# Edge attention of a graph layer: weights read from PSUM, two steps weighed by ScalarE, the bias added by TensorE

## The chip, the cores and the metric

The kernel runs on one core of a Trainium2 chip. The metric is the device time of one execution in microseconds. Times are in microseconds (us) unless marked ns. PE is TensorE, DVE VectorE, ACT ScalarE, POOL GpSimd, and SP the queue of SyncE.

## The reference, cut to what matters

Four layers follow each other: attention over the edges of a graph, a mixture of experts, a relational graph layer, and a second mixture. The change is in the first one only. Its nodes have 256 features in 8 heads, and there are 100,000 edges, sorted by destination.

```python
q = (nfeat @ Wq.T).reshape(n, HEADS, HEAD_DIM) / SCALING
k = (nfeat @ Wk.T).reshape(n, HEADS, HEAD_DIM)
v = (nfeat @ Wv.T).reshape(n, HEADS, HEAD_DIM)
attn = jnp.einsum('ehd,ehd->eh', k[src], q[dst])
attn = attn + attn_bias
m = jax.ops.segment_max(attn, dst, num_segments=n)
a = jnp.exp(attn - m[dst])
s = jax.ops.segment_sum(a, dst, num_segments=n)
a = a / s[dst]
out = jax.ops.segment_sum(v[src] * a[:, :, None], dst, num_segments=n)
return out.reshape(n, FEAT) @ Wo.T
```

## The kernel before

`attention_layer` works on steps of 128 edges, one edge per partition. Sixteen steps are a group (IT), two steps a pair (so 8 PAIRS in a group), and there are 55 groups (G). The instructions are written out by hand for each engine, and engines wait for each other by semaphores alone. There are 57 periods. In period k three groups are in work at once:

- group k: the products of keys and queries and their sums per head (`product`, `sum_heads`);
- group g = k-1: the bias, the running maxima over edges of one destination, and the exponential (`add_bias`, `scan_ahead`, `scan_back`, `chain_rows`, `maxima`, `factor`);
- group c = k-2: the values times the weights, summed per destination and added to the nodes (`weigh`, `sum_pair`, `add`, `rescale`).

POOL gathers the keys and values of each step by an indirect DMA (L278): 16 in a group, into `KV`, which has room for three groups. A buffer is refilled pair by pair, as soon as `sum_pair` has read it. DVE's `product` waits for the gathers four steps at a time.

PE turns the one-hot masks (`turn_masks`), fetches the queries of a pair by a matmul into the PSUM tensor `QP` (`dst_rows`, L379), of which there are three (BANKS = 3), so that `dst_rows` of pair v waits for the product of pair v-3. It turns the scores of a group into the PSUM tensor T (L404), and the exponentials into W (L433), which lies in the same PSUM bank CH as T and the small rows and columns of the softmax. `sum_pair` (L391) sums the weighed values of a pair.

DVE goes through the eight pairs of a period in the order of the loop in its `body`. For each pair: `product` (L454), then what that pair has of the softmax chain, then one `weigh` (L471), then `sum_heads` (L463), then `add` (L493). `weigh` is three pairs ahead of `add` (LEAD = 3): pairs 0 to 2 of the next group are weighed at pair 7, the first of them after a wait for `w_copied`. `add_bias` (L500) adds the bias to T and writes TB in SBUF, which the scan (L505) and `maxima` (L535) read. `weigh` multiplies two steps of values in `KV` by the weights that ACT has copied there.

ACT makes the masks (`distances`, L308, and `masks`, L317), moves them (`to_sbuf`, `move_masks`), and takes the exponential EX (L339) when `maxima` is done; after PE has turned it, ACT copies the weights from W to the last 8 columns of each step in `KV` (L343). `sum_pair` reads these columns too, as the sum of the weights. All of this stands in one order on ACT: what follows the wait for `neg` follows all masks ahead of it.

SP loads runs, bias and links of group k when `maxima` of group k-3 is done.

Of the kernel before, what the change touches and what calls it, by code (L numbers as in the profile page):

```python
# [190 lines left out]
def attention_layer(nc, m, d):  # L191
# [4 lines left out]
    PERIODS = G + 2  # L196
    RING = 3
    QUADS = IT // 4
    BANKS = 3
    LEAD = 3  # L200
    SUMS = 2
    ROW = 2 * FEAT + HEADS
    assert BANKS == RING and PAIRS % BANKS == 2
    with ExitStack() as ctx:
        s = sems(nc, m, "attn", "staged far masks turned turned_sb q_rows product reduced st_turned biased scan rows row_sums rows_l "
                 "cols most neg exp w_turned w_copied rows_f fac_in fac_out fac_less factor rescaled rescale weighted moved sums added "
                 "cleared")
        kv_in = [[new_sem(nc, m, f"attn_kv_in{i}_{q}") for q in range(QUADS)] for i in range(RING)]
        runs_in = [new_sem(nc, m, f"attn_runs_in{i}") for i in range(RING)]
        sb = lambda nm, sh, dt: ctx.enter_context(nc.sbuf_tensor(f"attn_{nm}", sh, dt))  # L210
# [3 lines left out]
        far = sb("far", [P, 4, P], F32)  # L214
        OHT = sb("OHT", [P, IT, P], F32)
        ST = sb("ST", [P, HEADS * IT], F32)
        TB = sb("TB", [P, P], F32)
        A = sb("A", [P, P], F32)
        B = sb("B", [P, P], F32)
        EX = sb("EX", [P, P], F32)  # L220
# [10 lines left out]
        QP = [ctx.enter_context(nc.psum_tensor(f"attn_QP{i}", [P, 2 * FEAT], F32)) for i in range(BANKS)]  # L231
        CH = ctx.enter_context(nc.psum_tensor("attn_CH", [P, 512], F32))
        SP = [ctx.enter_context(nc.psum_tensor(f"attn_SP{i}", [P, 512], F32)) for i in range(SUMS)]
        T, W = CH[:, 0:P], CH[:, P:2 * P]
        row_f, row_l = CH[0:1, 2 * P:3 * P], CH[0:1, 3 * P:4 * P]
        col_f, col_l, pfac = CH[:, P:P + 1], CH[:, P + 1:P + 2], CH[:, 2 * P:2 * P + HEADS]
        query = lambda blk: m.node[:, bass.ds(blk * NUMC + NUMC, FEAT)]
# [7 lines left out]
        with nc.Block() as block:  # L245
# [38 lines left out]
            @block.scalar  # L284
            def _(act):
                def restage(k, i):
                    if has(k, G):
                        act.copy(stage[:, i * IT:(i + 1) * IT], m.idx_src[:, bass.ds(k * IT, IT)]).then_inc(s["staged"], 1)

                def to_sbuf(k, q):  # L290
                    if has(k, G):

                        need(act, s["q_rows"], (k - 1) * PAIRS + (2 * q + 2))
                        act.wait_ge(s["turned"], k * QUADS + (q + 1))
                        act.copy(OHT[:, 4 * q:4 * q + 4, :].rearrange("p a b -> p (a b)"), TP[q % 2][:, 0:512]).then_inc(s["turned_sb"], 1)

                def move_masks(k, i, q):
                    if has(k, G):

                        act.wait_ge(s["reduced"], k * PAIRS + (2 * q + 2))  # L300
                        act.copy(KV[:, i * IT + 4 * q:i * IT + 4 * q + 4, 0:P], OHB[:, 4 * q:4 * q + 4, :]).then_inc(s["moved"], 1)

                def distances(k, q):
                    if has(k, G):

                        need(act, s["masks"], k * QUADS + q)
                        for n in range(4):
                            act.activation(far[:, n, :], m.iota_f[:, :], ACT.Abs, scale=-1.0,  # L308
                                           bias=m.dst_in[:, bass.ds(k * IT + 4 * q + n, 1)]).then_inc(s["far"], 1)

                def masks(k, q):
                    if has(k, G):

                        need(act, s["moved"], (k - 1) * QUADS + (q + 1))
                        need(act, s["turned"], (k - 1) * QUADS + (q + 1))
                        act.wait_ge(s["far"], k * IT + (4 * q + 4))
                        act.activation(OHB[:, 4 * q:4 * q + 4, :], far[:, :, :], ACT.Relu, scale=-1.0, bias=1.0).then_inc(s["masks"], 1)  # L317

                def body(k, i, turn):
                    g, j = k - 1, (i + 2) % 3  # L320
                    to_sbuf(k, 2)
                    if has(g, G):

                        for q in range(QUADS):
                            act.wait_ge(kv_in[j][q], landed(turn, j != 2) * (16 * 4))
                    restage(k + 2, j)
                    distances(k, 3)
                    move_masks(k, i, 0)
                    masks(k, 3)
                    distances(k + 1, 0)  # L330
                    to_sbuf(k, 3)
                    masks(k + 1, 0)
                    distances(k + 1, 1)
                    move_masks(k, i, 1)
                    masks(k + 1, 1)
                    to_sbuf(k + 1, 0)
                    if has(g, G):
                        act.wait_ge(s["neg"], g + 1)
                        act.activation(EX[:, :], B[:, :], ACT.Exp, scale=-1.0).then_inc(s["exp"], 1)  # L339
                        act.wait_ge(s["fac_in"], g + 1)  # L340
                        act.activation(fac[0:1, 2, :], fac[0:1, 1, :], ACT.Exp, scale=-1.0).then_inc(s["fac_out"], 1)
                        act.wait_ge(s["w_turned"], g + 1)
                        act.copy(KV[:, j * IT:(j + 1) * IT, 2 * FEAT:ROW], W.rearrange("p (h s) -> p s h", s=IT)).then_inc(s["w_copied"], 1)  # L343
                    distances(k + 1, 2)
                    move_masks(k, i, 2)
                    to_sbuf(k + 1, 1)
                    masks(k + 1, 2)
                    if has(g, G):
                        act.wait_ge(s["factor"], g + 1)
                        act.copy(FAC[:, :], pfac).then_inc(s["rescaled"], 1)  # L350
                    move_masks(k, i, 3)

                for n in range(2):
                    restage(n, n)
                for q in range(3):
                    distances(0, q)
                    masks(0, q)
                for q in range(2):
                    to_sbuf(0, q)
                every_period(act, body, PERIODS)  # L360

            @block.tensor
            def _(pe):
# [9 lines left out]
                def dst_rows(k, i, blks, v):  # L373
                    if has(k, G) and v < PAIRS:
# [1 line left out]

                        need(pe, s["product"], k * PAIRS + (v + 1 - BANKS))
                        for u in (2 * v, 2 * v + 1):
                            mm = pe.matmul(QP[(2 * i + v) % BANKS][:, (u % 2) * FEAT:(u % 2 + 1) * FEAT], OHT[:, u, :], query(blks[v]),  # L379
                                           start=True, stop=True)  # L380
                        mm.then_inc(s["q_rows"], 1)

                def sum_pair(c, j, v):
                    if has(c, G):
                        pe.wait_ge(s["weighted"], c * PAIRS + (v + 1))
                        if v % 2 == 0:
                            pe.wait_ge(s["moved"], c * QUADS + (v // 2 + 1))

# [6 lines left out]
                def body(k, i, turn):  # L395
# [4 lines left out]
                    if has(g, G):  # L400
                        pe.wait_ge(s["reduced"], (g + 1) * PAIRS)

                        need(pe, s["rescaled"], g)
                        pe.transpose(T, ST[:, :], m.ident[:, :]).then_inc(s["st_turned"], 1)  # L404
                    dst_rows(k, i, to, 1)
                    sum_pair(c, n, 0)
                    turn_masks(k, 2)
# [22 lines left out]
                    if has(g, G):  # L430
                        pe.wait_ge(s["rows_f"], 3 * g + 3)
                        pe.wait_ge(s["exp"], g + 1)
                        pe.transpose(W, EX[:, :], m.ident[:, :]).then_inc(s["w_turned"], 1)  # L433
                    turn_masks(k + 1, 1)
                    sum_pair(c, n, 7)
# [11 lines left out]
            def _(dve):  # L447
                def product(k, i, turn, v):
                    if has(k, G):
                        if v % 2 == 0:  # L450
                            dve.wait_ge(kv_in[i][v // 2], (turn + 1) * (16 * 4))
                        dve.wait_ge(s["q_rows"], k * PAIRS + (v + 1))
                        keys = KV[:, i * IT + 2 * v:i * IT + 2 * v + 2, 0:FEAT]
                        dve.tensor_tensor(keys, keys, QP[(2 * i + v) % BANKS][:, :].rearrange("p (s c) -> p s c", c=FEAT),  # L454
                                          ALU.mult).then_inc(s["product"], 1)

                def sum_heads(k, i, v):
# [7 lines left out]
                                          AX.X, ALU.add).then_inc(s["reduced"], 1)  # L465

                def weigh(c, j, v):
                    if has(c, G) and v < PAIRS:
                        at = j * IT + 2 * v
                        rows = KV[:, at:at + 2, FEAT:2 * FEAT].rearrange("p s (a b) -> p s a b", b=DH)  # L470
                        dve.tensor_tensor(rows, rows, KV[:, at:at + 2, 2 * FEAT:ROW].unsqueeze(3).to_broadcast([P, 2, HEADS, DH]),  # L471
                                          ALU.mult).then_inc(s["weighted"], 1)

                def rescale(c, blks):
# [18 lines left out]
                        dve.scalar_tensor_tensor(acc, acc, m.same[:, bass.ds(c * IT + 2 * v, 1)], SP[v % SUMS][:, 0:NUMC],  # L493
                                                 ALU.mult, ALU.add).then_inc(s["added"], 1)

                def add_bias(g, j, turn):
                    if has(g, G):
                        dve.wait_ge(runs_in[j], landed(turn, j != 2) * (16 * 5))
                        dve.wait_ge(s["st_turned"], g + 1)
                        dve.tensor_tensor(TB[:, :], T, bias[:, j, :], ALU.add).then_inc(s["biased"], 1)  # L500

                def scan_ahead(g, j):
                    if has(g, G):
                        dve.wait_ge(s["biased"], g + 1)
                        dve.tensor_tensor_scan(A[:, :], runs[:, j, 0:P], TB[:, :], -BIG, ALU.add, ALU.max).then_inc(s["scan"], 1)  # L505

                def scan_back(g, j):
                    if has(g, G):
# [13 lines left out]
                def maxima(g, j):  # L522
                    if has(g, G):
# [8 lines left out]
                        dve.scalar_tensor_tensor(B[:, :], runs[:, j, 2 * P:3 * P], col_l, B[:, :], ALU.add, ALU.max).then_inc(s["most"], 1)  # L532
                        dve.tensor_scalar(fac[0:1, 1, :], old, FLOOR, None, ALU.max).then_inc(s["rows_f"], 1)
                        dve.wait_ge(s["most"], 2 * g + 2)
                        dve.scalar_tensor_tensor(B[:, :], B[:, :], FLOOR, TB[:, :], ALU.max, ALU.subtract).then_inc(s["neg"], 1)  # L535
                        dve.wait_ge(s["rows_f"], 3 * g + 2)
                        dve.scalar_tensor_tensor(fac[0:1, 1, :], fac[0:1, 0, :], FLOOR, fac[0:1, 1, :], ALU.max, ALU.subtract).then_inc(s["fac_in"], 1)
                        dve.scalar_tensor_tensor(old, ahead[0:1, IT - 1::IT], lw[0:1, j, HEADS * IT:HEADS * IT + 1],
# [15 lines left out]
                def body(k, i, turn):  # L554
# [3 lines left out]
                    for v in range(PAIRS):  # L558
                        product(k, i, turn, v)
                        if v == 0:  # L560
                            add_bias(g, j, turn)
                            rescale(c, blks)
                        if v == 1:
                            scan_ahead(g, j)
# [2236 lines left out]
```

## Time and profile before

| | |
|---|---|
| median of 3 runs | 4223.15 us (4221.75 to 4224.39) |
| the profiled execution, its own time | 4219.4 us |
| its span | 4217.6 us |
| mean granted clock of PE over the span | 0.889 |
| attention layer, first gather to last weighing | 178.5 to about 1404 us |
| busy over the span | PE 83%, DVE 67%, POOL 55%, ACT 46% |

The shares of the span are means over stages that differ. The layer that is changed is the stretch from about 178 to 1406 us, some 29% of the span, and it is read by itself below. A busy time of POOL in this stretch is the time of the gathers' instructions alone; the time between them is shown as idle, released by "issue" when the profile shows nothing that the engine waited for.

### The profile page before, as it was taken

What the parts mean: (1) busy time and instruction counts of PE and PEld (TensorE: products, weight loads), DVE (VectorE), ACT (ScalarE), POOL (GpSimd) and SP (SyncE); (2) the same over time, 40 slices, a digit from 0 to 9 for tenths busy, and PEclk for the clock granted to TensorE, in tenths of its full rate; (3) what the DMA queues carried; (4) which work ended last, traced back from release to release, by engine and by line L of the source; (5) the groups of instructions that cost most, each with busy time, mean ns of one, the idle gap of its engine ahead of it and who ended that gap; (6) DMA issues with size and microseconds to landing.
All of it is one profiled execution on the core that took longest, in us unless ns stands there. A gap on an engine that the chain in (4) does not pass through costs nothing. (4 is left out here: it accounts for less than half of the span.)

```text
span 4217.6 us, 67721 instructions
## 1 busy us (share of the span) xinstructions
PE 3496.7 (83%) x17983; PEld 2727.1 (65%) x17984; DVE 2818.7 (67%) x7798; ACT 1935.8 (46%) x5274; POOL 2319.3 (55%) x2470
## 2 busy tenths in 40 slices
PE   8788888888888799799989997877878777866793
PEld 4466666666666699799975444655656555645692
DVE  5499999999999655411112222888888888875456
ACT  2355555555555233233322334666666666636230
POOL 5477777777777155400002222777777777737441
PEclk9899999999999999899999998788887888765896
DMA  6677777777777411111113445555565556534446
GB/s 190 200 210 203 202 206 205 207 205 201 203 207 205 151 40 40 56 35 37 35 55 150 178 178 195 170 175 171 168 178 170 168 168 176 160 107 147 122 133 217
DMA packets 266461, 656.43 MB, mean 156 GB/s; under 512 B 52764, under 2 KB 140984, under 8 KB 250408
## 3 DMA queue, kind: packets, MB, share of 16 engines
q0 software_dynamic: 128768, 394.47, 33.2%
q1 hardware_dynamic: 130328, 251.92, 17.4%
q10 hardware_dynamic: 7056, 6.43, 0.4%
q8 instruction: 132, 2.16, 0.2%
q14 instruction: 177, 1.45, 0.1%
HBM read 521.34 MB, written 131.29 MB: 155 GB/s over the span
## 5 line engine op out<-in xcount | busy, mean ns | idle before, releaser
L278 POOL DMA_INDIRECT attn_KV<-kv_tab,attn_stage x880 | 930.1, 1057 | 279.6 <-issue 252.1
L1846 POOL DMA_INDIRECT rel_V<-h_tab,rel_stage x880 | 833.9, 948 | 309.0 <-issue 229.6
L1949 PE MATMUL rel_SP<-rel_V,rel_OH 128*128 128x264 f32 x1760 | 608.5, 483 | 3.6 <-DVE node L2018 1.7
L379 PE MATMUL attn_QP<-node,attn_OHT 128*128 x1760 | 507.4, 414 | 10.2 <-issue 5.5
L391 PE MATMUL attn_SP<-attn_KV 128*128 128x264 f32 x1760 | 494.7, 407 | 20.9 <-DVE node L493 20.3
L1949 PEld LDWEIGHTS rel_SP<-rel_V,rel_OH 128*128 128x128 f32 x1760 | 372.6, 233 | 75.7 <-ACT rel_OH L1884 10.5
L391 PEld LDWEIGHTS attn_SP<-attn_KV 128*128 128x128 f32 x1760 | 344.9, 201 | 94.8 <-issue 37.7
L2018 DVE TENSOR_TENSOR node<-node,rel_SP 128x264 f32 x880 | 366.0, 416 | 50.5 <-PE rel_SP L1949 28.2
L379 PEld LDWEIGHTS attn_QP<-node,attn_OHT 128*128 128x128 f32 x1760 | 334.1, 203 | 61.3 <-issue 14.6
L1740 PE MATMUL pr_H<-WX,pr_YT 128*128 128x512 f32 x784 | 345.3, 593 | 0.0
L454 DVE TENSOR_TENSOR attn_KV<-attn_KV,attn_QP 128x512 f32<-128x512 f32 x440 | 298.0, 677 | 56.0 <-DMA attn_KV<-kv_tab,attn_stage 55.9
L463 DVE TENSOR_REDUCE attn_ST<-attn_KV 128x16 f32<-128x512 f32 x440 | 297.7, 677 | 0.3
L1641 POOL DMA_INDIRECT pr_R<-r_tab,pr_row_of x49 | 49.1, 1002 | 450.6 <-DVE pr_row_of L1699 431.4
L2024 DVE TENSOR_TENSOR rel_V<-rel_V,rel_WB 128x512 f32<-128x512 f32 x440 | 295.7, 673 | 0.0
L471 DVE TENSOR_TENSOR attn_KV<-attn_KV 128x512 f32<-128x512 f32 x440 | 293.6, 677 | 0.0
L1937 PEld LDWEIGHTS rel_QP<-sd,rel_OHT 128*128 128x128 f32 x1760 | 264.9, 224 | 33.2 <-issue 19.6
L308 ACT ACTIVATE attn_far<-iota_f,dst_in 128x128 f32<-128x128 f32 x880 | 281.1, 391 | 3.6
L1937 PE MATMUL rel_QP<-sd,rel_OHT 128*128 x1760 | 266.5, 303 | 15.2 <-ACT rel_OHT L1867 14.9
L1875 ACT ACTIVATE rel_far<-iota_f,dst_in 128x128 f32<-128x128 f32 x880 | 278.5, 388 | 0.0
L1523 ACT ACTIVATE exp_HT<-exp_HB,b 128x128 f32<-128x128 f32 x448 | 127.7, 368 | 301.5 <-PE exp_HB L1461 301.5
L1565 DVE TENSOR_TENSOR exp_R<-exp_RB,exp_bd 128x256 f32<-128x256 f32 x56 | 23.8, 424 | 360.4 <-PE exp_RB L1540 360.4
L1740 PEld LDWEIGHTS pr_H<-WX,pr_YT 128*128 128x128 f32 x784 | 145.7, 191 | 164.4 <-issue 164.4
(393 smaller groups left out, 6761.0 us busy)
## 6 DMA issues: line engine op xcount, KB each, us to landing
rel_OHT<-dst_rows SPq DMA_DIRECT2D x55, 1024.0 KB
h_tab<-pr_H SPq DMA_DIRECT2D x49, 1056.0 KB, 4.0
attn_KV<-kv_tab,attn_stage POOLq DMA_INDIRECT x880, 3.8
rel_V<-h_tab,rel_stage POOLq DMA_INDIRECT x880
pair_Y<-y SPq DMA_DIRECT2D x105, 130.0 KB, 2.1
kv_tab<-qkv_KV SPq DMA_DIRECT2D x49, 256.0 KB, 2.5
mix_Y<-y_out SPq DMA_DIRECT2D x49, 256.0 KB, 4.3
attn_runs<-runs SPq DMA_DIRECT2D x55, 192.0 KB
```

The source lines that it names most:

```text
L278: pool.indirect_dma_start(out=KV[:, i * IT + u, 0:2 * FEAT], out_offset=None, in_=d["kv_tab"][:, :], in_offset=bass.IndirectOffsetOnAxis(a ...
L379: mm = pe.matmul(QP[(2 * i + v) % BANKS][:, (u % 2) * FEAT:(u % 2 + 1) * FEAT], OHT[:, u, :], query(blks[v]), start=True, stop=True)
L391: mm = pe.matmul(SP[v % SUMS][:, 0:NUMC], KV[:, j * IT + u, 0:P], KV[:, j * IT + u, FEAT:ROW], start=(u % 2 == 0), stop=(u % 2 == 1))
L454: dve.tensor_tensor(keys, keys, QP[(2 * i + v) % BANKS][:, :].rearrange("p (s c) -> p s c", c=FEAT), ALU.mult).then_inc(s["product"], 1)
L463: dve.tensor_reduce(ST[:, :].rearrange("p (h s) -> p s h", s=IT)[:, 2 * v:2 * v + 2, :], KV[:, i * IT + 2 * v:i * IT + 2 * v + 2, 0:FEAT]. ...
L471: dve.tensor_tensor(rows, rows, KV[:, at:at + 2, 2 * FEAT:ROW].unsqueeze(3).to_broadcast([P, 2, HEADS, DH]), ALU.mult).then_inc(s["weighte ...
L1740: mm = pe.matmul(HP[g][:, :], f.YT[:, i, k * P:(k + 1) * P], WX[:, k, g * 512:(g + 1) * 512], start=(k == 0), stop=(k == 1))
L1846: pool.indirect_dma_start(out=V[:, i * IT + u, :], out_offset=None, in_=d["h_tab"][:, :], in_offset=bass.IndirectOffsetOnAxis(ap=stage[:, ...
L1937: mm = pe.matmul(QP[q // 2][:, (u % 8) * RH:(u % 8 + 1) * RH], OHT[:, k % 2, u, :], m.sd[:, bass.ds(blks[u // 2] * RH, RH)], start=True, s ...
L1949: pe.matmul(SP[(c * IT + u) % SUMS][:, 0:NUMC], OH[:, j * IT + u, :], V[:, j * IT + u, :], start=True, stop=True).then_inc(s["sums"], 1)
L2018: dve.tensor_tensor(acc, acc, SP[(c * IT + u) % SUMS][:, 0:NUMC], ALU.add).then_inc(s["added"], 1)
L2024: dve.tensor_tensor(rows, rows, weights[:, 2 * v:2 * v + 2, :].unsqueeze(3).to_broadcast([P, 2, HEADS, DH]), ALU.mult).then_inc(s["weighte ...
```

## The change

- The weights W get a PSUM bank of their own (WB). DVE's `weigh` reads the weights from PSUM, through a view of W, and no longer from `KV`. The copy of the weights into `KV` and DVE's wait for it (`w_copied`) stay. PE turns the next exponentials into W only when DVE's weighings of the group before are done.
- To free that bank, `QP` has two tensors and no longer three: `dst_rows` of pair v waits for the product of pair v-2.
- DVE weighs pairs 0 to 6 (OWN = 7). The last pair, steps 14 and 15, is weighed by ACT, with 16 activations (2 steps x 8 heads), each over 128 partitions x 32 columns in place, with the weight as a scale per partition. They stand after `masks(k + 1, 0)` in ACT's order.
- `add_bias` is gone from DVE, and TB with it. PE multiplies the scores by the identity into T and, after a wait for the bias's load, adds the bias by a second matmul with the identity into the same T. The scan and `maxima` read T in PSUM.

```diff
-    BANKS = 3
+    BANKS = 2
+    OWN = PAIRS - 1
...
-        T, W = CH[:, 0:P], CH[:, P:2 * P]
+        WB = ctx.enter_context(nc.psum_tensor("attn_WB", [P, 512], F32))
+        T, W = CH[:, 0:P], WB[:, 0:P]
+        weights = W.rearrange("p (h s) -> p s h", s=IT)
...
+                def weigh_last(c, j):
+                    if has(c, G):
+                        for u in (IT - 2, IT - 1):
+                            at = j * IT + u
+                            for h in range(HEADS):
+                                mm = act.activation(KV[:, at, FEAT + h * DH:FEAT + (h + 1) * DH],
+                                                    KV[:, at, FEAT + h * DH:FEAT + (h + 1) * DH], ACT.Identity,
+                                                    scale=KV[:, at, 2 * FEAT + h:2 * FEAT + h + 1])
+                        mm.then_inc(s["last_weighted"], 1)
...
                     masks(k + 1, 0)
+                    if has(k - 2, G):
+                        act.wait_ge(s["w_copied"], k - 1)
+                    weigh_last(k - 2, (i + 1) % 3)
                     distances(k + 1, 1)
...
-                            mm = pe.matmul(QP[(2 * i + v) % BANKS][:, (u % 2) * FEAT:(u % 2 + 1) * FEAT], OHT[:, u, :], query(blks[v]),
+                            mm = pe.matmul(QP[v % BANKS][:, (u % 2) * FEAT:(u % 2 + 1) * FEAT], OHT[:, u, :], query(blks[v]),
...
-                        pe.wait_ge(s["weighted"], c * PAIRS + (v + 1))
+                        if v < OWN:
+                            pe.wait_ge(s["weighted"], c * OWN + (v + 1))
+                        else:
+                            pe.wait_ge(s["last_weighted"], c + 1)
...
-                        pe.transpose(T, ST[:, :], m.ident[:, :]).then_inc(s["st_turned"], 1)
+                        pe.matmul(T, ST[:, :], m.ident[:, :], start=True, stop=False).then_inc(s["st_turned"], 1)
+                        pe.wait_ge(runs_in[j], landed(turn, j != 2) * (16 * 5))
+                        pe.matmul(T, m.ident[:, :], bias[:, j, :], start=False, stop=True).then_inc(s["biased"], 1)
...
                         pe.wait_ge(s["exp"], g + 1)
+
+                        need(pe, s["weighted"], g * OWN)
                         pe.transpose(W, EX[:, :], m.ident[:, :]).then_inc(s["w_turned"], 1)
...
-                    if has(c, G) and v < PAIRS:
+                    if has(c, G) and v < OWN:
                         at = j * IT + 2 * v
                         rows = KV[:, at:at + 2, FEAT:2 * FEAT].rearrange("p s (a b) -> p s a b", b=DH)
-                        dve.tensor_tensor(rows, rows, KV[:, at:at + 2, 2 * FEAT:ROW].unsqueeze(3).to_broadcast([P, 2, HEADS, DH]),
+                        dve.tensor_tensor(rows, rows, weights[:, 2 * v:2 * v + 2, :].unsqueeze(3).to_broadcast([P, 2, HEADS, DH]),
                                           ALU.mult).then_inc(s["weighted"], 1)
...
-                        dve.tensor_tensor(TB[:, :], T, bias[:, j, :], ALU.add).then_inc(s["biased"], 1)
...
-                        dve.tensor_tensor_scan(A[:, :], runs[:, j, 0:P], TB[:, :], -BIG, ALU.add, ALU.max).then_inc(s["scan"], 1)
+                        dve.tensor_tensor_scan(A[:, :], runs[:, j, 0:P], T, -BIG, ALU.add, ALU.max).then_inc(s["scan"], 1)
...
-                        dve.scalar_tensor_tensor(B[:, :], B[:, :], FLOOR, TB[:, :], ALU.max, ALU.subtract).then_inc(s["neg"], 1)
+                        dve.scalar_tensor_tensor(B[:, :], B[:, :], FLOOR, T, ALU.max, ALU.subtract).then_inc(s["neg"], 1)
```

## Rows read from the trace of the kernel before

**Rows 1.** Windows: us, busy PE, PEld, DVE, ACT, POOL, clock, DMA

```profile
600.00:900.00 300.00, 253.34 (x1210) 193.25 (x1210) 291.41 (x664) 169.92 (x455) 232.92 (x221) 0.95 0.72 205
```

**Rows 2.** The gather's line, 300 to 1300 us, who waits

```profile
L278 POOL DMA_INDIRECT attn_KV<-kv_tab,attn_stage x732: 946/948/1895, 299.8 to 1299.4; - x183
...
  issue: 208.8, 685
...
  DVE attn_KV L454: 29.7, 40
```

**Rows 3.** Groups by line, POOL, 178 to 222 and 2700 to 3300

```profile
L278 POOL DMA_INDIRECT attn_KV<-kv_tab,attn_stage x35 | 33.3, 951 | 22.1 <-ACT attn_stage L288 11.7 <-issue 10.4
...
L1846 POOL DMA_INDIRECT rel_V<-h_tab,rel_stage x480 | 454.4, 947 | 146.2 <-issue 124.9 <-PE rel_SP L1949 21.3
```

**Rows 4.** Timeline (start, us), DVE, one instruction of each period

```profile
221.72 0.42 DVE L544 TENSOR_SCALAR attn_fac<-attn_fac 1x8 f32<-1x8 f32 x1
...
1361.08 0.35 DVE L544 TENSOR_SCALAR attn_fac<-attn_fac 1x8 f32<-1x8 f32 x1
...
1382.12 0.15 DVE L544 TENSOR_SCALAR attn_fac<-attn_fac 1x8 f32<-1x8 f32 x1
```

**Rows 5.** Timeline, DVE and POOL, 704 to 720 us

```profile
704.67 0.68 DVE L471 TENSOR_TENSOR attn_KV<-attn_KV 128x512 f32<-128x512 f32 x1
...
705.28 0.68 DVE L463 TENSOR_REDUCE attn_ST<-attn_KV 128x16 f32<-128x512 f32 x1
...
708.60 0.28 DVE L500 TENSOR_TENSOR attn_TB<-attn_CH,attn_bias 128x128 f32<-128x128 f32 x1
...
708.80 0.42 DVE L480 SCALAR_TENSOR_TENSOR node<-attn_FAC,node 128x256 f32 x1
...
713.99 0.95 POOL L278 DMA_INDIRECT attn_KV<-kv_tab,attn_stage  x1 [0.30 <-issue]
...
714.37 0.68 DVE L471 TENSOR_TENSOR attn_KV<-attn_KV 128x512 f32<-128x512 f32 x1
...
715.24 0.95 POOL L278 DMA_INDIRECT attn_KV<-kv_tab,attn_stage  x1 [0.30 <-issue]
...
719.19 1.88 POOL L278 DMA_INDIRECT attn_KV<-kv_tab,attn_stage  x1 [0.30 <-issue]
...
719.57 0.67 DVE L471 TENSOR_TENSOR attn_KV<-attn_KV 128x512 f32<-128x512 f32 x1
```

**Rows 6.** Timeline, the softmax chain and ScalarE, 700 to 723 us

```profile
700.92 0.29 DVE L535 SCALAR_TENSOR_TENSOR attn_B<-attn_B,attn_TB 128x128 f32<-128x128 f32 x1
...
702.03 0.27 ACT L343 COPY attn_KV<-attn_CH 128x128 f32<-128x128 f32 x1 [0.38 <-PE attn_CH L433]
...
716.99 1.28 ACT L308 ACTIVATE attn_far<-iota_f,dst_in 128x128 f32<-128x128 f32 x4
...
718.68 0.62 ACT L301 CAST attn_KV<-attn_OHB 128x512 f32<-128x512 bf16 x1 [0.42 <-DVE attn_ST L463]
...
722.87 0.31 ACT L339 ACTIVATE attn_EX<-attn_B 128x128 f32<-128x128 f32 x1 [2.43 <-DVE attn_B L535]
```

**Rows 7.** Groups by line and form, ScalarE, whole span

```profile
L308 ACT ACTIVATE attn_far<-iota_f,dst_in 128x128 f32<-128x128 f32 x880 | 281.1, 391 | 3.6
...
L317 ACT ACTIVATE attn_OHB<-attn_far 128x512 bf16<-128x512 f32 x220 | 138.3, 628 | 1.8
...
L2279 ACT ACTIVATE route_Y<-node,route_shift,route_rstd 128x256 f32<-128x256 f32 x49 | 29.2, 597 | 54.8 <-DVE route_shift L2470 54.8
...
L339 ACT ACTIVATE attn_EX<-attn_B 128x128 f32<-128x128 f32 x55 | 17.0, 309 | 112.1 <-DVE attn_B L535 112.1
```

**Rows 8.** Timeline, PE and its readers, 720 to 724 us

```profile
720.87 1.03 PE L379 MATMUL attn_QP<-node,attn_OHT 128*128 x4
...
721.17 0.67 DVE L454 TENSOR_TENSOR attn_KV<-attn_KV,attn_QP 128x512 f32<-128x512 f32 x1
...
724.00 0.67 DVE L454 TENSOR_TENSOR attn_KV<-attn_KV,attn_QP 128x512 f32<-128x512 f32 x1
```

More of the change, by code:

```diff
@@ L198, in attention_layer @@
     QUADS = IT // 4
-    BANKS = 3
+    BANKS = 2
     LEAD = 3
+    OWN = PAIRS - 1
     SUMS = 2
     ROW = 2 * FEAT + HEADS
-    assert BANKS == RING and PAIRS % BANKS == 2
+    assert PAIRS % BANKS == 0
     with ExitStack() as ctx:
@@ L206, in attention_layer @@
                  "cols most neg exp w_turned w_copied rows_f fac_in fac_out fac_less factor rescaled rescale weighted moved sums added "
-                 "cleared")
+                 "cleared last_weighted")
         kv_in = [[new_sem(nc, m, f"attn_kv_in{i}_{q}") for q in range(QUADS)] for i in range(RING)]
@@ L216, in attention_layer @@
         ST = sb("ST", [P, HEADS * IT], F32)
-        TB = sb("TB", [P, P], F32)
         A = sb("A", [P, P], F32)
@@ L453, in product @@
                         keys = KV[:, i * IT + 2 * v:i * IT + 2 * v + 2, 0:FEAT]
-                        dve.tensor_tensor(keys, keys, QP[(2 * i + v) % BANKS][:, :].rearrange("p (s c) -> p s c", c=FEAT),
+                        dve.tensor_tensor(keys, keys, QP[v % BANKS][:, :].rearrange("p (s c) -> p s c", c=FEAT),
                                           ALU.mult).then_inc(s["product"], 1)
@@ L494, in add @@
                                                  ALU.mult, ALU.add).then_inc(s["added"], 1)
[L496 to L499, printed above, removed]
-                        dve.tensor_tensor(TB[:, :], T, bias[:, j, :], ALU.add).then_inc(s["biased"], 1)
                 def scan_ahead(g, j):
@@ L560, in body @@
                         if v == 0:
-                            add_bias(g, j, turn)
                             rescale(c, blks)
```

## The prediction

> **What bounds the kernel now.** I read the windows first. In the changed layer DVE is busy for 291.41 of 300 us, POOL for 232.92, PE for 253.34 and ACT for 169.92 [rows 1]. That looks like a kernel bound by DVE. The gather's own line says something else. Between 300 and 1300 us it has 732 instructions; idle time of POOL before them is given to "issue" 685 times, 208.8 us or 0.30 us each, and DVE waited for their landing 40 times, 29.7 us in all [rows 2]. So POOL never rests: it is always in a gather or between two. Their median is 948 ns, the longest took 1895 [rows 2]; 732 in 1000 us is one every 1.366 us, 0.30 of it between them, so the mean took 1.06 us. Sixteen make a period of 16 x 1.366 = 21.86 us.
>
> The timeline of DVE gives the same period. The one instruction L544 of each period starts at 221.72 us the first time and at 1382.12 the last but one time, 53 periods later: 1160.40 / 53 = 21.89 us [rows 4]. The shortest period, 1361.08 to 1382.12, is 21.04 [rows 4]: there DVE waited for nobody. So DVE has 21.04 us of work and POOL 21.89, and the difference of 0.85 is waiting: 0.65 of it for a gather to land (29.7 us in 45.7 periods). Both must be shortened for the period to fall.
>
> Why is a gather ever longer than 948 ns? The timeline shows which are. The one at 719.19 took 1.88 us, and DVE weighed beside it from 719.57; the one at 715.24 had sums, an add and a product beside it and took 0.95. Not every meeting costs: that at 713.99 also took 0.95, with a weighing from 714.37 [rows 5]. The same line, before the first weighing (178 to 222 us, 35 gathers, with products, sums and scans on DVE), has a mean of 951 ns, and the relational layer, whose weighing reads its weights from PSUM, gathers 480 times at a mean of 947 [rows 3]. `weigh` is here the one long instruction of DVE with both inputs in SBUF; the product reads one from PSUM.
>
> **The weighing from PSUM.** What it takes away is the excess of the gathers. POOL's period becomes 16 x (0.95 + 0.30) = 20.0 us, 1.9 less. DVE's weighing keeps its length: the product, which has the same size and one input in PSUM, took 0.67 [rows 8], and `weigh` 0.68 [rows 5]. Bounds: if the weighing holds up gathers as before, the excess falls only with the one weighing of eight that goes (below); if nothing holds them up, 20.0.
>
> The Trainium skill (SBUF — State Buffer, Who interferes with whom) speaks both ways: a DVE instruction with two SBUF inputs contends with a GpSimd instruction that reads SBUF, but a tensor_tensor was seen not to stall such a DMA, since its descriptors need the write interface (inferred there). By the second, the excess would have another cause and stay, which is the rival of no effect below. The trace bears out the first, by the rows just given.
>
> **What DVE loses.** One weighing of eight: from the start of L471 to that of the next instruction is 705.28 - 704.67 = 0.61 us [rows 5]. `add_bias`: 708.80 - 708.60 = 0.20 [rows 5]. The scan and `maxima` read T from PSUM in place of TB; product and weighing show no difference between the two memories, so I take 0, bounds -0.05 and +0.05. DVE: 21.04 - 0.61 - 0.20 = 20.23 us. It is now the longer of the two, by 0.23.
>
> **What ACT gains.** Sixteen activations of 32 columns with a pointer as scale; the trace has none. An activation of 128 columns without a pointer took 309 ns and one of 512 took 628: 0.83 ns a column. L308, 128 columns and one pointer, took 391 [rows 7], and four of them in a row 1.28 us, so they follow each other by (1.28 - 0.39) / 3 = 0.30 [rows 6]. With 96 columns fewer the spacing is 0.30 - 0.08 = 0.22 us: 16 x 0.22 = 3.5 us a period. ACT is busy 57% of the time [rows 1], 12.4 of 21.9 us, and would have 15.9 of 20.4. The upper bound is L2279, with two pointers, 597 ns for 256 columns [rows 7]: less 224 columns 0.41, nothing overlapped, 16 x 0.41 = 6.6 us. The lower bound is a little over 0.1 (309 less 80 less the overlap of 0.1), 2 us. I take 3.5, since L308 has the same kind of operand.
>
> The place matters more than the sum. The activations stand ahead of `distances(k + 1, 1)` (716.99), and behind these stand the masks and then EX, whose input DVE gives. ACT has slack there: it idled 0.42 us before 718.68 and 2.43 before EX at 722.87, 2.85 in all [rows 6]. That input comes 0.6 us earlier after the change, since the weighing that goes lies between. So EX starts 3.5 - 2.85 + 0.6 = 1.25 us later than it could. Who waits for it? PE turns it, ACT copies it, and DVE's first weighing waits for the copy. Before, the input's instruction started at 700.92, the copy ended at 702.30 [rows 6] and that weighing started at 704.67 [rows 5]: 2.37 us of slack, of which 1.1 is left. No stall. It would begin at (3.5 + 1.1) / 16 = 0.29 us an activation. Behind EX on PE are masks, the last `sum_pair` and `dst_rows` of the next period; each has over 1 us in the rows around 702 to 708, and I put nothing down for them.
>
> **What PE gains.** T was one transpose; now two float32 matmuls of 128 columns. A pair of 256 columns took 1.03 us for four pieces [rows 8], about 0.22 apart, so four pieces of 128 columns cost 0.5 to 0.9, and 0.3 to 0.7 more than now. The wait for the bias holds nothing: SP issued it two periods before. The scan comes more than a whole pair later on DVE. PE is busy 84% of 21.9 us [rows 1], 18.4, and would be for 18.9 of 20.4.
>
> **Two banks for the queries.** `dst_rows` of pair 7 started at 720.87; its new condition, the product of pair 5, ended at 721.17 + 0.67 = 721.84 [rows 8], so it starts about 1 us later at the most. It was needed at 724.00 [rows 8] and would be ready at 722.9. The gap before it is the longest pair (`maxima`), so this hides too. After the change pairs 4 and 6 are short ones on DVE (product, sums, add: 1.6 us) against 1.8 for PE's two matmul pairs; a lag that PE has from a stretch at 1.2 GHz (its granted clock here has a mean of 0.95 [rows 1], which is a tenth of the time at the lower level) will now sometimes show on DVE. POOL's lateness hid it before. I allow 0.17 us a period, bounds 0 and 0.5.
>
> **The sum.** Period 20.23 + 0.17 = 20.40, saved 21.89 - 20.40 = 1.49, times 53 = 79 us. The last two periods have no gathers, and DVE's own 0.8 goes once there in full: 1 us. Together 80. The profiled execution's own time is 4219.4, so 4139.4; the median of the runs lies 3.75 above it, so 4143 us.
>
> **Rivals.**
> - A part is lost (0.15): EX comes later than counted, or PE's shorter lead shows, and DVE stalls 0.4 to 1.2 us a period. For it: three slacks become one thin one at the same time. Against it: each is over 1 us by the rows. In the middle, period 21.2, saved 37, 4187 us.
> - The weighing still holds up the gathers (0.05). The excess of 1.87 keeps 7/8: period 20.0 + 1.64 = 21.64, saved 0.25 x 53 = 13, 4210 us. Against it, the relational layer's 947 ns.
> - No effect (0.03): the excess has nothing to do with DVE: 21.87, about 4222 us.
> - Slower (0.06): the activations make ACT's order the chain. From 0.29 us each, DVE waits at its first weighing, and the gain is eaten at 0.29 + 1.49 / 16 = 0.38. At 0.41 the period is 20.4 + 16 x 0.12 = 22.3, and the time 53 x 0.43 = 23 us more, 4246. For it: no row shows an activation with a pointer as its scale and alone. Against it: L308's spacing.
> - Better than the sum (0.01): DVE shortens by the scans too, and POOL's 20.0 is the bound: saved 100, 4123 us.
>
> **The numbers.** The likeliest case has 0.70: 20.23 to 20.70 a period, 4128 (with the scans' 0.05) to 4160 us. The range of 8 in 10 takes in two thirds of the partial loss: 4128 to 4190. Measurements of this kernel tell 0.2%, 8 us, from no change. Faster by over that: 0.70 + 0.15 + 0.05 + 0.01 = 0.91, of which I take 0.01 off since 4210 is near the bound; same 0.04; slower 0.06.
>
> **What would show it.** Right: gathers at 946 to 955 ns mean in the stretch; waits of POOL for `sum_pair` appear, because it now runs ahead of DVE; DVE's waits for a gather are gone; L544 every 20.3 to 20.6 us; the new activations 0.22 us apart; EX released by ACT's own order. Wrong: gathers still over 1.0 us (the contention isn't the weighing's inputs), DVE idle before its first `weigh` (ACT), or before products and adds (PE).

## The result and the profile after

The changed kernel takes 4147.49 us (median of 4 runs, 4144.23 to 4149.77) against 4222.45 us before: a ratio of 0.9821, 95% interval 0.9804 to 0.9838. Predicted were 4143 us. Measured once more, the same two kernels took 4146.64 and 4225.36 us, ratio 0.9810 (0.9797 to 0.9824). The profiled execution took 4149.8 us, its span 4148.0.

The windows of the changed kernel, with the columns of [rows 1]:

```profile
600.00:900.00 300.00, 264.58 (x1341) 200.75 (x1341) 298.97 (x679) 227.83 (x727) 226.86 (x239) 1.00 0.77 221
```

DVE now has no idle time to speak of (298.97 of 300 us, 291.41 before), PE's granted clock in the layer is 1.00 where it was 0.95, and ACT is busy for 227.83 us in place of 169.92.

The gather's line (a line number of this kernel), 300 to 1300 us, and what POOL was idle for, to be held against [rows 2]:

```profile
L280 POOL DMA_INDIRECT attn_KV<-kv_tab,attn_stage x785: 944/946/1213, 299.3 to 1289.4; - x197
...
  issue: 231.3, 739
...
  PE attn_SP L409: 12.8, 42
```

There are 785 gathers in the same 1000 us in place of 732; the median is 946 ns and the longest 1213, where it had been 1895. Under "who waited for it" this answer has no line any more: DVE never waits for a gather to land. One sign that the prediction named hardly shows: POOL's waits for `sum_pair` (L409) are 12.8 us at 42 places, 0.30 each, which is the usual time between two gathers, and the kernel before had 14.3 us at 47.

The one instruction of each period, in DVE's timeline, the first and the 54th, as in [rows 4]:

```profile
223.07 0.15 DVE L560 TENSOR_SCALAR attn_fac<-attn_fac 1x8 f32<-1x8 f32 x1
...
1304.77 0.15 DVE L560 TENSOR_SCALAR attn_fac<-attn_fac 1x8 f32<-1x8 f32 x1
```

(1304.77 - 223.07) / 53 = 20.41 us a period; it was 21.89. The 53 periods took 1160.4 us and take 1081.7, 79 us less, and the layer from its first gather to its last `add` is shorter by as much (1228.4 us before, 1149.2 now). The whole was 75 us shorter the first time and 79 the second. In the spans of the two profiled executions the difference is 69.6: the stages behind the layer, which have the same code, took 2819.1 us from the last `add` to the end of the span, where they had taken 2810.7. That difference isn't explained; the repeated run below says a little more.

A stretch of one period in the timeline of the changed kernel, where L310 is the new weighing on ACT, L476 the product, L485 the sum, L551 the input of EX, L354 EX, L356 the small exponential for the factor, L358 the copy of the weights, L560 `factor`, L493 DVE's weighing, L394 the queries' matmuls, L385 the turning of the masks:

```profile
707.02 3.48 ACT L310 ACTIVATE attn_KV<-attn_KV 128x32 f32<-128x32 f32 x16
...
709.13 0.67 DVE L476 TENSOR_TENSOR attn_KV<-attn_KV,attn_QP 128x512 f32<-128x512 f32 x1
...
709.83 0.69 DVE L485 TENSOR_REDUCE attn_ST<-attn_KV 128x16 f32<-128x512 f32 x1
...
712.21 0.29 DVE L551 SCALAR_TENSOR_TENSOR attn_B<-attn_B,attn_CH 128x128 f32<-128x128 f32 x1
...
713.22 0.31 ACT L354 ACTIVATE attn_EX<-attn_B 128x128 f32<-128x128 f32 x1
...
713.42 0.19 ACT L356 ACTIVATE attn_fac<-attn_fac 1x8 f32<-1x8 f32 x1
...
713.97 0.27 ACT L358 COPY attn_KV<-attn_WB 128x128 f32<-128x128 f32 x1 [0.35 <-PE attn_WB L455]
...
714.29 0.35 DVE L560 TENSOR_SCALAR attn_fac<-attn_fac 1x8 f32<-1x8 f32 x1
...
716.00 0.68 DVE L493 TENSOR_TENSOR attn_KV<-attn_KV,attn_WB 128x512 f32<-128x512 f32 x1
...
722.32 1.13 PE L394 MATMUL attn_QP<-node,attn_OHT 128*128 x4 [0.49 <-DVE attn_KV L476]
...
725.27 0.40 PE L385 MATMUL attn_TP<-ident_b,attn_OHB 128*128 128x128 bf16 x4 [0.72 <-ACT attn_OHB L329]
```

Sixteen activations took 3.48 us, the last one's own 0.31 included: (3.48 - 0.31) / 15 = 0.211 us apart. EX starts 1.01 us after the start of its input's instruction; it is ACT's own order now that releases it. Before the change it was 0.33, from the line below to EX at 722.87 [rows 6]. The copy of the weights ends at 714.24, and the first weighing starts at 716.00. PE waits 0.49 us for a product before `dst_rows`, which is the shorter lead of two banks, and only 0.72 us for the masks. Its wait for masks had been 90.1 us at 46 places between 300 and 1300 us.

The input of EX in the kernel before (L535 there is L551 here):

```profile
722.54 0.29 DVE L535 SCALAR_TENSOR_TENSOR attn_B<-attn_B,attn_TB 128x128 f32<-128x128 f32 x1
```

The waits of the same kernel, 300 to 1300 us (total us, times, longest):

```profile
POOL attn_KV L280 <- issue: 231.3, 739, 1.3
...
PE attn_QP L394 <- DVE attn_KV L476: 45.4, 98, 0.5
...
PE attn_TP L385 <- ACT attn_OHB L329: 35.6, 49, 0.8
```

No wait of DVE is among them.

### The profile page after: what moved, and what is told of

It reads as the page before. It is cut to its first block and busy times, and to the rows that moved or that the text cites. A ratio compares the mean times of both kernels' runs of the same rounds, so it can differ in the third digit from the quotient of the medians.

```text
span 4148.0 us, 68767 instructions
## 1 busy us (share of the span) xinstructions
PE 3473.8 (84%) x18148; PEld 2705.6 (65%) x18149; DVE 2773.1 (67%) x7688; ACT 2103.1 (51%) x6154; POOL 2226.9 (54%) x2470
## 5 line engine op out<-in xcount | busy, mean ns | idle before, releaser
L280 POOL DMA_INDIRECT attn_KV<-kv_tab,attn_stage x880 | 836.7, 951 | 285.7 <-issue 259.4
L394 PE MATMUL attn_QP<-node,attn_OHT 128*128 x1760 | 487.2, 400 | 62.7 <-DVE attn_KV L476 56.7
L409 PE MATMUL attn_SP<-attn_KV 128*128 128x264 f32 x1760 | 467.5, 389 | 1.3 <-DVE node L515 1.3
L394 PEld LDWEIGHTS attn_QP<-node,attn_OHT 128*128 128x128 f32 x1760 | 304.8, 192 | 148.4 <-issue 117.2
L409 PEld LDWEIGHTS attn_SP<-attn_KV 128*128 128x128 f32 x1760 | 330.3, 191 | 52.2 <-issue 2.3
L476 DVE TENSOR_TENSOR attn_KV<-attn_KV,attn_QP 128x512 f32<-128x512 f32 x440 | 297.5, 676 | 23.7 <-DMA attn_KV<-kv_tab,attn_stage 23.2
L485 DVE TENSOR_REDUCE attn_ST<-attn_KV 128x16 f32<-128x512 f32 x440 | 298.2, 678 | 2.2
L493 DVE TENSOR_TENSOR attn_KV<-attn_KV,attn_WB 128x512 f32<-128x512 f32 x385 | 254.2, 672 | 0.0
```

Of the source, the lines that this page charges most:

```text
L280: pool.indirect_dma_start(out=KV[:, i * IT + u, 0:2 * FEAT], out_offset=None, in_=d["kv_tab"][:, :], in_offset=bass.IndirectOffsetOnAxis(a ...
L394: mm = pe.matmul(QP[v % BANKS][:, (u % 2) * FEAT:(u % 2 + 1) * FEAT], OHT[:, u, :], query(blks[v]), start=True, stop=True)
L409: mm = pe.matmul(SP[v % SUMS][:, 0:NUMC], KV[:, j * IT + u, 0:P], KV[:, j * IT + u, FEAT:ROW], start=(u % 2 == 0), stop=(u % 2 == 1))
L476: dve.tensor_tensor(keys, keys, QP[v % BANKS][:, :].rearrange("p (s c) -> p s c", c=FEAT), ALU.mult).then_inc(s["product"], 1)
L485: dve.tensor_reduce(ST[:, :].rearrange("p (h s) -> p s h", s=IT)[:, 2 * v:2 * v + 2, :], KV[:, i * IT + 2 * v:i * IT + 2 * v + 2, 0:FEAT]. ...
```

## The experiments

All of them change `attention_layer` alone. "Layer's period" is worked out as above, from the first and the 54th `factor` of the profiled execution.

| kernel | time, us | before on the same chip | ratio (95%) | period, us |
|---|---|---|---|---|
| before | 4222.5 | | | 21.89 |
| changed | 4147.5 | 4222.5 | 0.9821 (0.9804-0.9838) | 20.41 |
| e1 weights from SBUF again | 4163.9 | 4221.6 | 0.9859 (0.9836-0.9882) | 20.88 |
| e2 weights from PSUM alone | 4178.6 | 4221.6 | 0.9899 (0.9883-0.9916) | 21.04 |
| e3 DVE weighs all pairs | 4169.8 | 4221.6 | 0.9876 (0.9860-0.9893) | 20.83 |
| e4 bias on DVE | 4154.5 | 4221.6 | 0.9839 (0.9823-0.9856) | 20.59 |
| changed, repeated | 4146.6 | 4225.4 | 0.9810 (0.9797-0.9824) | 20.41 |
| e8 pair 6 weighed later | 4138.4 | 4225.4 | 0.9794 (0.9781-0.9808) | 20.27 |
| e9 and a third step on ACT | 4126.5 | 4225.4 | 0.9764 (0.9751-0.9777) | 20.15 |
| e5 two banks alone | 4673.2 | 4672.4 | 1.0001 (0.9992-1.0011) | - |
| e6 eight activations more | 4687.3 | 4672.4 | 1.0038 (1.0024-1.0051) | - |
| e7 sixteen activations more | 4697.1 | 4672.4 | 1.0054 (1.0037-1.0072) | - |
| f6 as e6 | 4200.7 | 4225.6 | 0.9936 (0.9920-0.9953) | 21.42 |
| f7 as e7 | 4330.7 | 4225.6 | 1.0246 (1.0229-1.0263) | 23.9 |

**e1, the weights read from SBUF again.**

```diff
-                        dve.tensor_tensor(rows, rows, weights[:, 2 * v:2 * v + 2, :].unsqueeze(3).to_broadcast([P, 2, HEADS, DH]),
+                        dve.tensor_tensor(rows, rows, KV[:, at:at + 2, 2 * FEAT:ROW].unsqueeze(3).to_broadcast([P, 2, HEADS, DH]),
```

> The changed kernel, but DVE's weighing reads the weights from the copy in KV (SBUF) again; everything else of the change stays. Theory (a weighing with both inputs in SBUF lengthens the gathers): the gathers' mean goes from 0.95 back to 1.04-1.06 us, POOL is the bound again with a period of about 21.6 us, and the time is 4147 + 53 x 1.25 = about 4213 us. Rival (the excess had another cause, and DVE's shorter work made the gain): gathers stay at 0.95 us, period 20.4, time 4147 us.

Its gathers by line and by source, 300 to 1200 us:

```profile
L280 POOL DMA_INDIRECT attn_KV<-kv_tab,attn_stage x693 | 690.7, 997 | 211.2 <-issue 198.7 <-PE attn_SP L409 12.5
```

```profile
L280 POOL DMA_INDIRECT attn_KV<-kv_tab,attn_stage x693: 946/947/1530, 299.2 to 1199.8; - x174
...
  DVE attn_KV L476: 15.8, 25
```

The direction is the theory's: the gathers' mean rises to 997 ns, the longest is 1530, and DVE waits for gathers again (15.8 us). The size is not: 4164 us where 4213 were expected, a mean of 0.997 where it was to be 1.04 to 1.06. The rival, no effect, is out: the four runs of e1 lie apart by more than usual (4156.8 to 4174.8 us), but all are above those of the changed kernel. Three meetings of a weighing (L493) and a gather in the timeline of e1 show what the size hangs on:

```profile
335.37 0.68 DVE L493 TENSOR_TENSOR attn_KV<-attn_KV 128x512 f32<-128x512 f32 x1
...
335.65 1.22 POOL L280 DMA_INDIRECT attn_KV<-kv_tab,attn_stage  x1 [0.30 <-issue]
...
338.35 0.67 DVE L493 TENSOR_TENSOR attn_KV<-attn_KV 128x512 f32<-128x512 f32 x1
...
338.43 1.41 POOL L280 DMA_INDIRECT attn_KV<-kv_tab,attn_stage  x1 [0.30 <-issue]
...
710.21 0.95 POOL L280 DMA_INDIRECT attn_KV<-kv_tab,attn_stage  x1 [0.30 <-issue]
...
710.33 0.68 DVE L493 TENSOR_TENSOR attn_KV<-attn_KV 128x512 f32<-128x512 f32 x1
```

The gathers at 335.65 and 338.43 began while a weighing was running, and took 1.22 and 1.41 us; they end about 0.8 us after the weighing did. The gather at 710.21 began 0.12 us before the weighing, and took its 0.95. I counted this over all gathers of the timeline between 300 and 1200 us. In e1, 153 of 692 began in a running weighing and took 1.17 us on average, the other 539 took 0.948. Before, 181 of 657 did and took 1.23; the others took 0.957, but for 23 that took twice a gather's time, 1.88, as the one at 719.19 [rows 5]. So one part of the price is set by how often a gather's start falls into a weighing, 4.4 times a period before and 3.5 in e1, and by how early in the weighing it falls. That depends on how the two engines' rhythms lie to each other, and I had no ground to carry 7/8 of the old excess over.

The other part are the 23. In the timeline each of them began during the product of pair 4, 0.38 to 0.39 us ahead of the weighing of pair 7. Of the 28 gathers that began at this place 23 took 1.88 us, while 28 that began as long ahead of the weighing of pair 5 took 0.95, as the one at 713.99 [rows 5]. e5 (below), which also weighs from SBUF, has the same: 27 of 29 ahead of pair 7's weighing, and none of 19 ahead of pair 5's. Pair 7 is the one that the change gives to ACT, so e1 lacks the place. Of the 78 us by which the 657 gathers before exceeded 0.946 us each, 22 belong to the weighing of pair 7. That is 29%, where the 7/8 had reckoned with one eighth. Why a gather is lengthened ahead of this weighing and not ahead of pair 5's is open.

**e2, the weights from PSUM alone.** The kernel before with W in a bank of its own and two query banks; DVE keeps all weighings and the bias. The diff is against the changed kernel.

```diff
-    OWN = PAIRS - 1
+    OWN = PAIRS
...
-                    weigh_last(k - 2, (i + 1) % 3)
...
-                        pe.matmul(T, ST[:, :], m.ident[:, :], start=True, stop=False).then_inc(s["st_turned"], 1)
-                        pe.wait_ge(runs_in[j], landed(turn, j != 2) * (16 * 5))
-                        pe.matmul(T, m.ident[:, :], bias[:, j, :], start=False, stop=True).then_inc(s["biased"], 1)
+                        pe.transpose(T, ST[:, :], m.ident[:, :]).then_inc(s["st_turned"], 1)
```

> The kernel before with one part of the change alone: the weights read from PSUM (W in a bank of its own, two query banks). DVE weighs all eight pairs and adds the bias itself. Theory: gathers at 0.95 us, so POOL would manage 20.0 us, and DVE's own 21.04 to 21.1 us is the bound: 4222 - 53 x 0.82 = about 4179 us. Rival (what counts is the work taken from DVE): no gain from this part, about 4222 us. Rival (two query banks cost): above 4190 us, with waits of DVE for PE.

Its windows and its gathers:

```profile
600.00:900.00 300.00, 258.23 (x1258) 190.98 (x1257) 299.52 (x684) 176.28 (x473) 218.69 (x229) 1.00 0.74 213
```

```profile
L281 POOL DMA_INDIRECT attn_KV<-kv_tab,attn_stage x692 | 663.6, 959 | 237.8 <-issue 187.2 <-PE attn_SP L407 50.7
```

4178.6 us, as expected to the microsecond. DVE is busy for 299.52 of 300 us and its period is 21.04, the shortest that it had before [rows 4]; POOL waits 50.7 us for `sum_pair`, since it is ahead now. The rivals are out: this part alone brings 43 us, and two query banks cost nothing that DVE could feel. The mean gather is 959 ns, not 948: other instructions of DVE with two inputs in SBUF are left. Of the 76 gathers over 1.0 us between 300 and 1200 us, 37 began during the first two wide instructions of `maxima`, 36 during scans with both inputs in SBUF, and 3 during `rescale`.

**e3, DVE weighs all pairs** (the first two edits of e2's diff, in the changed kernel).

> The changed kernel without ScalarE's weighing: DVE weighs all eight pairs, from PSUM. Theory (DVE is the bound after the change, and a weighing costs it 0.60 us, of which 0.10 was lost again because a sum now waits for its own product): period 20.37 + 0.50 = 20.87, 26 us more, about 4173 us. Rival (ScalarE's 16 activations hold the chain): nothing lost or even a gain, 4147 us or less.

Period 20.83, 4169.8 us: ACT's weighing is worth 0.42 us a period and 22 us, a little less than the 0.50 and 26 expected. The rival is out.

**e4, the bias on DVE** (the third edit of e2's diff, and `add_bias` with TB, in the changed kernel).

> The changed kernel with the bias added by DVE again (TB in SBUF, one transpose on PE). Theory (DVE is the bound and PE's two matmuls are hidden): 0.20 us more a period, 11 us, about 4158 us. Rival (TensorE's longer start of the period costs as much as DVE saves): 4147 us.

Period 20.59, 4154.5 us: the bias is worth 0.18 us a period, and 7 to 8 us, where 0.20 and 11 were expected. The rival is out.

**e5, two query banks alone, in the kernel before.**

```diff
-    BANKS = 3
+    BANKS = 2
...
-    ... QP[(2 * i + v) % BANKS] ...
+    ... QP[v % BANKS] ...
```

> The kernel before with two query banks in place of three, nothing else. Theory (the shorter lead is hidden): 4222 us, within 0.1%; PE shows waits for products. Rival (it costs by itself, and the rest of the change paid for it): over 4230 us with waits of DVE for the queries.

This kernel and e6 and e7 ran on a chip on which the kernel before takes 4672 us, 450 more than elsewhere, so their times stand only against that one. Its waits, 300 to 1200 us:

```profile
PEld attn_QP L379 <- issue: 114.7, 142, 4.2
...
DVE node L493 <- remote: 83.5, 46, 3.8
...
DVE node L493 <- PE attn_SP L391: 34.8, 36, 2.0
...
PE attn_QP L379 <- DVE attn_KV L454: 31.9, 26, 3.3
```

Two banks make no difference there either (1.0001). But PE's weight loads stand up to 4.2 us with nothing to wait for that the profile shows, and DVE's `add` (L493) waits up to 3.8 us, longest in total for something that the profile doesn't name ("remote"), and then for PE. That is another bound than the one that is studied here, and I don't know its cause.

**e6 and e7, more activations on ACT**, there, and **f6 and f7**, the same kernels on another chip.

```diff
                         mm.then_inc(s["last_weighted"], 1)
+                        for e in range(8):
+                            act.activation(spare[:, e, :], m.iota_f[:, 0:DH], ACT.Identity, scale=m.row_no[:, 0:1])
```

> The changed kernel with 8 activations of 128x32 with a scale pointer more a period on ScalarE, behind the 16, into a scrap tile: 8 x 0.21 = 1.7 us. In the changed kernel the copy of the weights ended 1.76 us before DVE's first weighing. Theory (that is the slack, and ScalarE isn't the bound): hardly a loss, 4147 to 4152 us. Rival (ScalarE's order already sets the period): 1.7 us more a period, 4237 us.

> The same with 16 more: 3.4 us. Theory: the slack of 1.76 is used up and DVE idles 1.6 us a period ahead of its first weighing: 53 x 1.6 = 85 us more, about 4232 us. Rival (slack larger than read, since DVE's idle time shifts what ScalarE waits for): well under 4200 us.

On the slow chip they took 1.0038 and 1.0054 of the time before. The changed kernel itself wasn't run there, so they say nothing of ACT's slack.

> The kernel of e6 once more, on another chip: where e5 to e7 ran, the kernel before took 4672 us and PE itself was late in both. 8 activations more a period are 1.7 us, and the changed kernel's slack was read as 1.76. Theory: 4147 to 4155 us. Rival (ScalarE's order sets the period): about 4237 us.

> The kernel of e7 once more, on another chip. 16 activations more a period are 3.4 us. Theory: 1.6 us of them come through at DVE's first weighing, 85 us, about 4232 us. Rival (slack larger than read): well under 4200 us.

f6: 53 us more than the changed kernel, where the theory had 0 to 8 and the rival 90. Both miss. Its timeline and its waits show who was first to feel it:

```profile
715.96 0.19 ACT L359 ACTIVATE attn_fac<-attn_fac 1x8 f32<-1x8 f32 x1
...
716.19 0.16 DVE L563 TENSOR_SCALAR attn_fac<-attn_fac 1x8 f32<-1x8 f32 x1 [1.06 <-ACT attn_fac L359]
```

```profile
DVE attn_fac L563 <- ACT attn_fac L359: 44.2, 42, 1.1
```

DVE waits at `factor` (L563 here), for the small exponential that ACT computes right after EX, and not at its first weighing. In the changed kernel that exponential ended at 713.42 + 0.19 = 713.61 and `factor` started at 714.29: a slack of 0.68 us, where I had counted 1.76 to the weighing. With it the sum closes: 8 x 0.211 = 1.69, less 0.68 is 1.01 us a period, and the period went from 20.41 to 21.42. (The median of this slack over all periods is 0.60, which gives 1.09, so it closes to 0.1 us.)

f7: 183 us more than the changed kernel, where the theory had 85; this misses too. By the same slack 3.38 - 0.68 = 2.70 us a period, 143 us; the period rose by 3.5. Its waits and a window hold the rest:

```profile
PE attn_WB L458 <- issue: 118.2, 37, 3.2
...
DVE attn_fac L563 <- ACT attn_fac L359: 101.8, 37, 2.8
...
DVE attn_KV L479 <- PE attn_QP L397: 18.5, 23, 0.8
```

```profile
600.00:900.00 300.00, 242.91 (x1141) 186.44 (x1140) 255.60 (x578) 236.28 (x826) 191.66 (x203) 0.92 0.66 190
```

DVE waits 2.75 us a period at `factor` (101.8 in 37), and 0.5 for the queries. PE idles up to 3.2 us here before it turns the weights, and its clock is 0.92.

**e8, pair 6 weighed later.** In the changed kernel the sum at 709.83 starts 0.70 us after its product at 709.13; everywhere else it is 0.60, with a weighing between.

```diff
-                        if v < PAIRS - LEAD:
+                        if v < PAIRS - LEAD - 2:
                             weigh(c, n, v + LEAD)
+                        if v == 4:
+                            weigh(c, n, 6)
```

> The changed kernel with DVE's weighing of pair 6 moved from pair 3's place to pair 4's, between the product and the sum that waits for it. Theory (DVE is the bound, and the sum of pair 4 follows its product 0.70 us after its start where others need 0.60, because nothing stands between the two): 0.10 us less a period, 5 to 6 us less, about 4142 us. Rival (that 0.10 is something else, or TensorE then waits for the weighing): no difference or slower.

Against the changed kernel on the same chip 8 us less, 4138.4 to 4146.6, and 0.14 us a period. A little more than expected; the rival is out.

**e9, and step 13 weighed by ACT.** e8, and in addition:

```diff
                     distances(k, 3)
+                    if has(k - 2, G):
+                        act.wait_ge(s["w_copied"], k - 1)
+                    weigh_last(k - 2, (i + 1) % 3, (IT - 3,), "step_weighted")
                     move_masks(k, i, 0)
...
+                        w = 1 if v == OWN - 1 else 2
```

> e8, and in addition step 13 weighed by ScalarE too, with 8 more activations at the place where it waits for the first sums of the period (it idled 2.1 us there); DVE's weighing of pair 6 has one step only. Theory: DVE's work falls by 0.10 + 0.27 to about 20.0 us, where POOL's 16 x 1.25 = 20.0 us is the bound again: period 20.05, about 16 us less than the changed kernel, 4131 us. DVE then waits for gathers to land again. Rival (ScalarE is full): EX or the masks come later, DVE idles ahead of its first weighing, 4140 us or more.

> The changed kernel once more, as the measure for the small differences of e8 and e9 on the same chip. Both theories: 4144 to 4150 us. The stages behind the attention layer, which nothing changed, were about 9 us longer in its profiled execution than in that of before; if that is a matter of the single execution, it moves here by some us.

The repeated kernel took 4146.6 us, as expected. What it was to show of the stages behind the layer came out against chance alone: they took 2817.0 us, 2 less than in the first profiled execution of the changed kernel, but still 6 more than in that of before. e2 has 2811.4 there, the other profiled executions on chips of this speed 2814.6 to 2818.7. The cause is open.

Windows and gathers of e9:

```profile
600.00:900.00 300.00, 270.67 (x1362) 202.66 (x1360) 298.11 (x689) 253.70 (x851) 227.16 (x240) 1.00 0.77 223
```

```profile
L280 POOL DMA_INDIRECT attn_KV<-kv_tab,attn_stage x717: 946/946/1225, 299.1 to 1199.0; - x180
...
  DVE attn_KV L481: 5.2, 11
```

4126.5 us, 20 less than the changed kernel and 99 less than the kernel before. More than half of the periods are below 20.0 us, the mean is 20.15, and DVE waits for gathers again (5.2 us), with 2 us of idle time in 300. POOL's rhythm is 900 / 717 = 1.255 us, 16 of them 20.1: both engines are nearly full, and the gathers are the bound again.

## Why the prediction was right, point by point

- **Two bounds close together.** Right, and what the rest rests on. e2 shows it from one side: with the gathers freed, DVE's 21.04 us bind. The other side, DVE's work taken away with the gathers still lengthened, is e1: its period is 20.88, and its shortest ones, in which DVE waits for nobody, are 20.35.
- **Gathers lengthened by weighings with two SBUF inputs.** Right in kind: e1 and the changed kernel differ in this one operand, 997 against 950 ns (746.1 us over 785 gathers). The Trainium skill (SBUF — State Buffer, Who interferes with whom) has both rules that were weighed; the first holds here, and its words that issue order decides who blocks agree with e1's timeline. They don't agree with the 23 gathers of the kernel before that began ahead of a weighing and took 1.88 us. The skill's sentence that a tensor_tensor was seen not to stall such a DMA does not hold in this kernel. The term that I mis-sized is the rival's price: 7/8 of the excess would stay, 1.64 us a period; e1 kept 0.8. The weighing that goes had 29% of the excess and not an eighth, and the starts of gathers fell less often, and later, into those that stay.
- **DVE's loss of work.** 0.20 for the bias: measured 0.18 (e4). 0.61 for the weighing: measured 0.42 (e3). Of the difference 0.10 comes back where a sum now follows its own product with nothing between (0.70 in place of 0.60). That was the largest cost on DVE that I had missed, and e8 takes it back. About 0.04 are short stalls that e3's timeline doesn't have: three short instructions (the second scan, and two on one partition in `maxima`) take 0.07 to 0.08 us longer in about ten of the 53 periods each. The rest is open. The scans and `maxima` read T from PSUM at no difference (409 and 288 ns by line, 415 and 292 before).
- **The allowance of 0.17** for PE's shorter lead. Its size was right by chance: the 0.10 is the larger part of it, and DVE has no wait for PE at all in the changed kernel. The allowance was made for a PE that lags at the lower clock, and the clock was 1.00; that the one follows from the other isn't shown.
- **ACT's sum.** 0.22 us an activation predicted, 0.211 measured; 3.5 us a period.
- **ACT's slack.** Wrong in its place. I followed EX to DVE's first weighing, reckoned 1.1 us left where 1.76 were, and passed over `factor`, which waits on the same chain and comes first (0.68 us left). It cost nothing here, but the threshold from which the change would have lost by ACT was 0.211 + 0.68 / 16 = 0.25 us an activation, not 0.29.
- **PE's two matmuls and two banks.** Hidden, as said: PE waits 0.46 us for the product at 98 places (45.4 us), DVE doesn't.
- **The sum.** Period 20.41 for 20.40, layer 79 us for 80, time 4147.5 for 4143. That the total fits to 4 us is in part luck. The profiled execution took 4149.8 us for 4139.4, since the stages behind the layer took 8 us more, which no term had; and the median, reckoned 3.75 us above the profiled execution, lies 2.3 below it.

Part by part the gains are 43 us for the weights from PSUM (e2), 9 for the bias on top (e3), and 22 for ACT's weighing on top of both. No run has them in another order. That the last two alone would have brought little while POOL was the bound is argued from the two periods, not shown.

## What to carry to other kernels

An engine that never rests need not look busy: count its instructions and the time between them ("issue"), and hold that period against the one of the engine that does. A DVE instruction whose second input moves from SBUF to PSUM can free a GpSimd engine that issues gathers, even where its own length stays the same. Before work is moved to an engine with slack, list everything that waits on the chain behind it, and take the first to wait, however small its instruction is.

## What the runs showed of the hardware that I had not expected

- A gather that begins while a DVE weighing with two SBUF inputs runs is lengthened to 1.17 to 1.23 us on average, and ends about 0.8 us after the weighing. One that begins ahead of the weighing kept its 0.95 in e1 (0.948 over 539). In the kernel before it did so too, but for one place of the period, where 23 of 28 that began 0.38 us ahead of the weighing took 1.88, just twice the usual; the reason is open.
- A DVE instruction that reads the result of the one right before it starts 0.70 us after it (709.13 to 709.83 in the changed kernel), where an independent one starts after 0.60 and the dependent one behind that loses nothing.
- PE's granted clock was 0.95 of 2.4 GHz with a wait for masks of 1.96 us a period (90.1 us at 46 places), and 1.00 with one of 0.73 (35.6 at 49); with up to 3.2 us idle once a period (f7) it was 0.92. That the wait sets the clock isn't shown.
- One chip of those used took 4672 us for the kernel before, 11% more than the others, and e5 there has PE's weight loads idle for up to 4.2 us with nothing to wait for that the profile shows; there the bound of this layer was another, and what the change does on it was not measured.
